# The order of the two score matmuls in a pair: turned scores first, plain scores second

## The chip, the cores and the metric

The kernel runs on one core of one Trainium2 chip. The metric is the device time of one execution in microseconds (us); the time before is the median of three runs. Five engines work in parallel and meet through semaphores: TensorE (PE in the profile; its weight loads have a row of their own, PEld), VectorE (DVE), ScalarE (ACT), GpSimd (POOL) and SyncE (SP), which here only starts DMAs.

## The reference

A transformer block on 16 sequences: an attention whose heads run along the channel axis, then a mixture of experts.

```python
# attention: x normalised over its last axis is q, ctx is k and v
qh = q.reshape(b, 8, 32, 512); kh = k.reshape(b, 8, 32, 512); vh = kh
s = SCALE * log(k_length)                      # one number per batch element
attn = softmax(s * einsum('bhdq,bhdk->bhqk', qh, kh), axis=-1)
x = x + einsum('bhqk,bhdk->bhdq', attn, vh).reshape(b, 256, 512)
# experts: normalise x, gate by softmax over 8 experts, take the top 2,
# relu(x @ w1[e]) @ w2[e] for at most C rows of each expert, weighed sum
x = x + moe(layernorm(x), Wg, w1, w2)
```

The softmax needs the maximum of each row of scores before it takes exponentials. This is why the kernel computes scores twice.

## The kernel before, in words

The attention has 32 groups (16 batch elements, two groups of 128 channels each, which are 4 heads of 32 dims). It runs in 32 steps `s`, software-pipelined over the groups:

- In step `s` the **plain** scores of group `s` are computed (queries on partitions, line 1086), 16 matmuls into a ring of three PSUM banks `ps_s`. VectorE takes the negated maximum of each (line 678), which frees the bank. The maxima are turned and sent by DMA as two extra rows into the operand `qst`.
- In the same step the **turned** scores of group `s-2` are computed (keys on partitions, line 1037), 16 matmuls into a ring of three banks `ps_t`. The extra rows subtract the maximum. ScalarE takes the exponential of each (line 460), which frees the bank.
- The exponentials are multiplied with the values (`ps_o`, line 1007, four matmuls side by side in 32-column strips) and with ones (`ps_l`, line 1013, four more) to give weighted values and sums. I call these eight the sums matmuls.

A step has four **blocks** `c` = 0 to 3 of four pairs `i` = 0 to 3. I write plain 0 to plain 3 and turned 0 to turned 3 for the matmuls of the pairs of one block. At the end of a block stand the sums matmuls for exponentials of the block before. Between pair 1 and pair 2 of a block something else may stand: in block 1 one matmul `shares` (line 1059, it takes the bank after plain 1 and waits for a small DMA `r_rows`), in block 2 the transposes of a row and of the values (lines 1044 and 1051, in the `ps_t` ring), in block 3 the gate logits (line 1109, in the `ps_s` ring) and, in odd steps from 7, the expert places (lines 1100, 1102).

The order of each engine's work is the order in which the code is written; nothing is scheduled by a planner. PE works strictly in this order. A plain matmul waits until the third-last use of the `ps_s` ring is read (`s_bank`), a turned one until the third-last use of the `ps_t` ring is read (`t_bank`). So in block 1 plain 2 waits for the maximum of plain 0, plain 3 for that of plain 1, because `shares` took a bank between them; and turned 3 waits for the exponential of turned 0. The first plain matmul of a step also waits for the DMAs that fill `qst` and `kst`, the first turned one for the DMAs with the maxima.

On ScalarE, between the exponentials of block 0 and those of block 1, stand two copies, `o_sb` from `ps_o` (line 475) and `l_sb` from `ps_l` (line 537), and then the issue of a DMA `l_wide` (line 541), which waits until `l_sb` is written. The copies wait for the sums matmuls at the end of block 0. On VectorE the maxima of a step are mixed with other short work: normalisation of a later group, the turning of the maxima, and in odd steps the choice of experts.

After step 31 a tail finishes the last two groups (turned scores only), and then the expert stage runs 16 tiles of 512 rows through `w1` and `w2`; neither has a pair that the change touches.

Of the kernel before, what the change touches and what calls it, by code (L numbers as in the profile page):

```python
# [51 lines left out]
def live(g):  # L52
    return 0 <= g < G


def pair_in(s):

    return s % 2 == 1 and 0 <= (s - 7) // 2 < B
# [45 lines left out]
def attention_and_dispatch(nc, x_rows, ctx_rows, klen, wg, out_rows, disp, totals, fill, spare,  # L104
                           w1, w2, raw, raw_ld, xin, first_ld, ident):
    s_turn, t_turn, (s_main, t_main) = bank_turns()
    with ExitStack() as stack:
# [130 lines left out]
        def turns(g, ring):  # L238

            return g // ring + 1  # L240
# [733 lines left out]
        def _(pe):  # L974
            def s_bank(k):

                if k > s_main + 2:
                    pe.wait_ge(s_free, k - 2)
                elif k > s_main:
                    pe.wait_ge(s_free, last_turn(k - s_main - 1, s_main))  # L980
                elif k > 3:
                    pe.wait_ge(s_free, k - 3)
                return s_at(k)

            def t_bank(k):

                if k > t_main + 4:
                    pe.wait_ge(t_free, k - 4)
                elif k == t_main + 4:
                    pe.wait_ge(s_free, last_turn(2, s_main))  # L990
                elif k > t_main:
                    pe.wait_ge(t_free, last_turn(k - t_main - 1, t_main))
                elif k > 3:
                    pe.wait_ge(t_free, k - 3)
                return t_at(k)

            def weighted(g, c):

                n = 4 * g + c
                pe.wait_ge(t_free, t_turn["t", g, c, HPG - 1])  # L1000
                if c == 0:
                    pe.wait_ge(t_free, t_turn["vt", g])
                    if g >= 1:
                        pe.wait_ge(o_saved, g)
                for h in range(HPG):
                    hd = slice(HD * h, HD * h + HD)
                    nc.tensor.matmul(ps_o[hd, :], vt[g % 4][:, c, hd], probs[n % 3][:, h, :],  # L1007
                                     start=(c == 0), stop=(c == NC4 - 1))
                if c == 0 and g >= 1:
                    pe.wait_ge(l_saved, g)  # L1010
                for h in range(HPG):
                    hd = slice(HD * h, HD * h + HD)
                    done = nc.tensor.matmul(ps_l[hd, :], ones[:, 0:HD], probs[n % 3][:, h, :],
                                            start=(c == 0), stop=(c == NC4 - 1))
                done.then_inc(pv_done, 1)
# [14 lines left out]
            def turned_logits(g, c, i):  # L1030
                cols = slice(P * c, P * c + P)
                if c == 0 and i == 0:
                    pe.wait_ge(mrow_ld[g % KR], (16 * 2 * NC4) * turns(g, KR))
                    if g < KR:
                        pe.wait_ge(ones_made, g + 1)
                bank = t_bank(t_turn["t", g, c, i])
                nc.tensor.matmul(bank[:], kst[g % KR][0:STACK + 2, i, cols],  # L1037
                                 qst[g % KR][0:STACK + 2, i, :], start=True, stop=True).then_inc(t_done, 1)

            def row_turned(g):  # L1040
                pe.wait_ge(x2_ready, g + 1)
                bank = t_bank(t_turn["x2t", g])
                for q in range(NC4):
                    done = nc.tensor.transpose(bank[:, P * q:P * q + P], xrow[:, g % RING, P * q:P * q + P], ident[:])
                done.then_inc(t_done, 1)

            def values(g):
                pe.wait_ge(c_ld[g % 4], 16 * turns(g, 4))
                bank = t_bank(t_turn["vt", g])
                for q in range(NC4):  # L1050
                    done = nc.tensor.transpose(bank[:, P * q:P * q + P], ct[g % 4][:, P * q:P * q + P], ident[:])
                done.then_inc(t_done, 1)

            def shares(g):
                pe.wait_ge(r_ld[g % 2], 32 * turns(g, 2))
                if g == 0:
                    pe.wait_ge(dims_st, 32)
                bank = s_bank(s_turn["r", g])
                nc.tensor.matmul(bank[:], to_dims[:], r_rows[g % 2][:], start=True, stop=True).then_inc(s_done, 1)
# [18 lines left out]
            for s in range(SLOTS):  # L1078
                for c in range(NC4):
                    for i in range(HPG):  # L1080
                        cols = slice(P * i, P * i + P)
                        if live(s):
                            if c == 0 and i == 0:
                                pe.wait_ge(stack_ld[s % KR], turns(s, KR) * (16 * COPIES))
                            bank = s_bank(s_turn["s", s, c, i])
                            nc.tensor.matmul(bank[:], qst[s % KR][0:STACK, c, cols], kst[s % KR][0:STACK, c, :],  # L1086
                                             start=True, stop=True).then_inc(s_done, 1)
                        if live(s - 2):
                            turned_logits(s - 2, c, i)
                        if i == 1 and c == 2 and live(s - 5):  # L1090
                            row_turned(s - 5)
                        if i == 1 and c == 2 and live(s - 1):
                            values(s - 1)
                        if i == 1 and c == 3 and (live(s - 5) or pair_in(s)):
                            bank = s_bank(s_turn["lp", s])
                            if pair_in(s):
                                n = (s - 7) // 2 + 1
                                pe.wait_ge(rt["before"], n)
                                pos = bank[:, 2 * E:4 * E]
                                nc.tensor.matmul(pos, earlier[:], picked[:].rearrange("p h e -> p (h e)"),  # L1100
                                                 start=True, stop=False)
                                done = nc.tensor.matmul(pos, ones[:], before[(n - 1) % 2][:].rearrange("p h e -> p (h e)"),
                                                        start=False, stop=True)
                            if live(s - 5):
                                pe.wait_ge(t_free, t_turn["x2t", s - 5])
                                if s == 5:
                                    pe.wait_ge(wg_ld, 16)
                                for q in range(NC4):
                                    done = nc.tensor.matmul(bank[:, 0:E], x2t[:, P * q:P * q + P], wg_sb[:, q, :],
                                                            start=(q == 0), stop=(q == NC4 - 1))  # L1110
                            done.then_inc(s_done, 1)
                        if i == 1 and c == 1 and live(s - 4):
                            shares(s - 4)
                    if c == 0 and live(s - 3):
                        weighted(s - 3, NC4 - 1)
                    if c > 0 and live(s - 2):
                        weighted(s - 2, c - 1)
# [742 lines left out]
```

## Time and profile before

| What | us |
|---|---|
| median of three runs | 2179.55 |
| lowest and highest run | 2177.81, 2179.68 |
| span of the profiled execution | 2177.8 |
| steady attention steps, from 80 to 605 | 525 |
| expert stage, from 681 to 2177 | 1496 |

The profile gives the span of the profiled execution, from the first to the last instruction; its own time is not listed apart from this, and the lowest run is as long as the span. Busy shares of the span: PE 97%, weight loads 70%, VectorE 46%, ScalarE 33%, GpSimd 22%. The granted TensorE clock was full (2.4 GHz) over nearly all of it.

How to read it. The start of a matmul and the time to the next start are sound; its duration is modelled and overlaps the next one, so a row of matmuls that reads 0.40 us each can follow at less than 0.25 us. A matmul needs its weight load first. When a load runs beside the matmul before, it is hidden; when it starts at the same time as its own matmul, the matmul's row is about 0.1 us longer (0.50), and that is the exposed load. The arrow names what ended an idle time.

### The profile page before, as it was taken

To read this page: it belongs to the slowest core of one execution; us is meant where nothing else is said; L and a number is where in the kernel's file an instruction comes from. 1 tells how busy PE (TensorE), PEld (TensorE's weight loads), DVE (VectorE), ACT (ScalarE), POOL (GpSimd) and SP (SyncE) were. 2 spreads that over 40 slices of the span, in tenths; PEclk is the share of its full clock that TensorE was granted. 3 is DMA by queue.
4 is the path that set the end of the run, shared out by engine and by line. 5 is a ranking of instruction groups with operands and counts; after the bars stand their busy time and mean duration, and the time that the engine had idled before them with its cause. 6 is when DMAs were issued, how large, how long until landed. Compare 5 with 4: busy or idle time off the path is not lost. (4 is left out here: it accounts for less than half of the span.)

```text
span 2177.8 us, 27085 instructions
## 1 busy us (share of the span) xinstructions
PE 2117.0 (97%) x10179; PEld 1518.8 (70%) x10179; DVE 1008.1 (46%) x1908; ACT 712.9 (33%) x1216; POOL 470.4 (22%) x593
## 2 busy tenths in 40 slices
PE   3999999999999999999999999999999999999997
PEld 1445454455547888878888887888888788888776
DVE  5677878878765434234324423423432342343211
ACT  1666666666652222113212212311311231132110
POOL 3334444343422111110301201031030102101101
PEclk9999999999999999999999999999999999999999
DMA  9876767776635435212613612422441252241101
GB/s 147 160 165 157 181 157 188 168 187 162 146 114 161 115 70 132 58 22 85 131 20 78 150 26 58 125 50 43 114 98 25 56 134 52 48 125 31 16 6 20
DMA packets 183895, 216.61 MB, mean 99 GB/s; under 512 B 39731, under 2 KB 111419, under 8 KB 183740
## 3 DMA queue, kind: packets, MB, share of 16 engines
q1 hardware_dynamic: 154128, 173.21, 34.1%
q0 software_dynamic: 22240, 37.92, 9.1%
q10 hardware_dynamic: 7372, 3.42, 0.7%
q8 instruction: 97, 1.59, 0.3%
q14 instruction: 58, 0.48, 0.1%
HBM read 113.93 MB, written 68.29 MB: 84 GB/s over the span
## 5 line engine op out<-in xcount | busy, mean ns | idle before, releaser
L1590 DVE SCALAR_TENSOR_TENSOR hlo<-ps_h,hhi 128x512 fp32r<-128x512 f32 x256 | 177.0, 692 | 928.4 <-ACT hhi L1467 928.4
L1467 ACT ACTIVATE hhi<-ps_h 128x512 fp32r<-128x512 f32 x256 | 152.9, 597 | 1123.4 <-PE ps_h L1731 1123.4
L1729 PE MATMUL ps_h<-xhi,w1hi 128*128 128x512 f32 x1024 | 404.9, 395 | 2.5 <-PEq L1316 1.3
L1748 PE MATMUL ps_y<-w2hi,hhi 128*128 128x512 f32 x1024 | 404.7, 395 | 0.7 <-DVE hlo L1590 0.7
L1749 PE MATMUL ps_y<-w2lo,hhi 128*128 128x512 f32 x1024 | 403.0, 394 | 1.0 <-issue 1.0
L1750 PE MATMUL ps_y<-w2hi,hlo 128*128 128x512 f32 x1024 | 403.7, 394 | 0.0
L1731 PE MATMUL ps_h<-xhi,w1lo 128*128 128x512 f32 x1024 | 403.6, 394 | 0.0
L1730 PE MATMUL ps_h<-xlo,w1hi 128*128 128x512 f32 x1024 | 403.0, 394 | 0.0
L678 DVE TENSOR_REDUCE nmax<-ps_s 128x1 f32<-128x512 f32 x512 | 335.7, 681 | 128.5 <-PE ps_s L1086 124.6
L460 ACT ACTIVATE probs<-ps_t 128x512 f32<-128x512 f32 x504 | 273.0, 604 | 183.1 <-PE ps_t L1037 145.8
L1729 PEld LDWEIGHTS ps_h<-xhi,w1hi 128*128 128x128 f32 x1024 | 192.3, 188 | 48.5 <-issue 3.9
L1749 PEld LDWEIGHTS ps_y<-w2lo,hhi 128*128 128x128 f32 x1024 | 193.1, 189 | 46.7 <-issue 1.5
L1730 PEld LDWEIGHTS ps_h<-xlo,w1hi 128*128 128x128 f32 x1024 | 193.0, 188 | 45.2
L1748 PEld LDWEIGHTS ps_y<-w2hi,hhi 128*128 128x128 f32 x1024 | 192.3, 188 | 46.0 <-DVE hlo L1590 1.1
L1731 PEld LDWEIGHTS ps_h<-xhi,w1lo 128*128 128x128 f32 x1024 | 192.3, 188 | 45.8
L1750 PEld LDWEIGHTS ps_y<-w2hi,hlo 128*128 128x128 f32 x1024 | 192.3, 188 | 45.8
L1086 PE MATMUL ps_s<-kst,qst 96*128 96x512 f32 x416 | 192.0, 472 | 30.5 <-DMA qst<-qlo 27.6
L1402 POOL DMA_INDIRECT out_x<-y,ids x64 | 103.3, 1614 | 453.6 <-DVE y L1632 439.0
L1086 PEld LDWEIGHTS ps_s<-kst,qst 96*128 96x128 f32 x416 | 81.7, 197 | 146.8 <-DVE nmax L678 76.7
L1037 PE MATMUL ps_t<-qst,kst 98*128 98x512 f32 x408 | 164.0, 406 | 1.9 <-DMA qst<-nturn 1.2
L1384 POOL TENSOR_TENSOR ids<-xtail,zeros 128x4 int32<-128x4 int32 x15 | 4.9, 328 | 712.8 <-DMA xtail<-dispatched 712.8
L1007 PE MATMUL ps_o<-probs,vt 128*32 128x512 f32 x1016 | 137.1, 612 | 3.3 <-ACT probs L460 3.3
(202 smaller groups left out, 2007.2 us busy)
## 6 DMA issues: line engine op xcount, KB each, us to landing
raw<-in_L_ffn_w SPq DMA_DIRECT2D x128, 512.0 KB, 4.9
qst<-qhi SPq DMA_DIRECT2D x64, 256.0 KB, 5.8
xin<-dispatched SPq DMA_DIRECT2D x60, 256.0 KB, 5.8
kst<-khi SPq DMA_DIRECT2D x52, 256.0 KB, 6.4
xt<-in_x SPq DMA_DIRECT2D x32, 256.0 KB, 3.1
ct<-in_ctx SPq DMA_DIRECT2D x32, 256.0 KB, 4.5
qst<-qlo SPq DMA_DIRECT2D x32, 256.0 KB, 6.8
xres<-in_x SPq DMA_DIRECT2D x32, 256.0 KB, 4.7
```

The lines of the kernel that those rows point to most:

```text
L460: nc.scalar.activation(probs[n % 3][:, i, :], t_at(k)[:], ACT.Exp).then_inc(t_free, 1)
L678: nc.vector.tensor_reduce(nmax[s % 2][:, i, c:c + 1], s_at(k)[:], AX, ALU.max, negate=True).then_inc(s_free, 1)
L1037: nc.tensor.matmul(bank[:], kst[g % KR][0:STACK + 2, i, cols], qst[g % KR][0:STACK + 2, i, :], start=True, stop=True).then_inc(t_done, 1)
L1086: nc.tensor.matmul(bank[:], qst[s % KR][0:STACK, c, cols], kst[s % KR][0:STACK, c, :], start=True, stop=True).then_inc(s_done, 1)
L1467: nc.scalar.activation(hhi[k % 2][:], ps_h[k % 3][:], ACT.Relu).then_inc(hhi_ready, 1)
L1590: nc.vector.scalar_tensor_tensor(hlo[k % 2][:], ps_h[k % 3][:], 0.0, hhi[k % 2][:].bitcast(F32), ALU.max, ALU.subtract).then_inc(h_ready, 1)
L1729: nc.tensor.matmul(to, w1hi[:, c, fs], xhi[n % 2][:, c, :], start=(c == 0), stop=False)
L1730: nc.tensor.matmul(to, w1hi[:, c, fs], xlo[n % 2][:, c, :], start=False, stop=False)
L1731: done = nc.tensor.matmul(to, w1lo[:, c, fs], xhi[n % 2][:, c, :], start=False, stop=(c == NC4 - 1))
L1748: nc.tensor.matmul(ps_y[b][:], hhi[k % 2][:, bs], w2hi[:, f, :], start=(f == 0), stop=False)
L1749: nc.tensor.matmul(ps_y[b][:], hhi[k % 2][:, bs], w2lo[:, f, :], start=False, stop=False)
L1750: done = nc.tensor.matmul(ps_y[b][:], hlo[k % 2][:, bs], w2hi[:, f, :], start=False, stop=(f == NF - 1))
```

## The change

In each pair of the step loop, the turned matmul now stands ahead of the plain one. The wait for `stack_ld` moves with the plain matmul. Nothing else is moved: the matmuls and transposes between pairs 1 and 2, and the sums matmuls at a block's end, stand where they stood; the rings' numbering is as before, since the two rings are counted apart. The other engines' programs are the same.

```diff
                         cols = slice(P * i, P * i + P)
+                        if live(s - 2):
+                            turned_logits(s - 2, c, i)
                         if live(s):
                             if c == 0 and i == 0:
                                 pe.wait_ge(stack_ld[s % KR], turns(s, KR) * (16 * COPIES))
                             bank = s_bank(s_turn["s", s, c, i])
                             nc.tensor.matmul(bank[:], qst[s % KR][0:STACK, c, cols], kst[s % KR][0:STACK, c, :],
                                              start=True, stop=True).then_inc(s_done, 1)
-                        if live(s - 2):
-                            turned_logits(s - 2, c, i)
```

PE in step 8, block 1, before. The numbers are buffer numbers: `ps_s1` is the second bank of the plain ring, `ps_t2` the third of the turned ring, `qst3` the operand of group 8, `qst1` that of group 6.

```order
L1013 MATMUL ps_l<-probs2,ones 32x512 x4
L1086 MATMUL ps_s1<-kst3,qst3 128x512
L1037 MATMUL ps_t2<-qst1,kst1 128x512
L1086 MATMUL ps_s2<-kst3,qst3 128x512
L1037 MATMUL ps_t0<-qst1,kst1 128x512
L1059 MATMUL ps_s0<-r_rows0,to_dims 128x512
L1086 MATMUL ps_s1<-kst3,qst3 128x512
L1037 MATMUL ps_t1<-qst1,kst1 128x512
L1086 MATMUL ps_s2<-kst3,qst3 128x512
L1037 MATMUL ps_t2<-qst1,kst1 128x512
L1007 MATMUL ps_o<-probs0,vt2 32x512 x4
```

The same place in the changed kernel:

```order
L1013 MATMUL ps_l<-probs2,ones 32x512 x4
L1037 MATMUL ps_t2<-qst1,kst1 128x512
L1088 MATMUL ps_s1<-kst3,qst3 128x512
L1037 MATMUL ps_t0<-qst1,kst1 128x512
L1088 MATMUL ps_s2<-kst3,qst3 128x512
L1059 MATMUL ps_s0<-r_rows0,to_dims 128x512
L1037 MATMUL ps_t1<-qst1,kst1 128x512
L1088 MATMUL ps_s1<-kst3,qst3 128x512
L1037 MATMUL ps_t2<-qst1,kst1 128x512
L1088 MATMUL ps_s2<-kst3,qst3 128x512
L1007 MATMUL ps_o<-probs0,vt2 32x512 x4
```

Each turned matmul moved one place up and each plain one down, within its pair. The block now begins with a turned matmul and has plain 3 between turned 3 and the sums matmuls. (Line 1086 of before is line 1088 after.)

PE in step 8, block 3, before:

```order
L1086 MATMUL ps_s1<-kst3,qst3 128x512
L1037 MATMUL ps_t0<-qst1,kst1 128x512
L1086 MATMUL ps_s2<-kst3,qst3 128x512
L1037 MATMUL ps_t1<-qst1,kst1 128x512
L1109 MATMUL ps_s0<-wg_sb,x2t 128x8 x4
L1086 MATMUL ps_s1<-kst3,qst3 128x512
L1037 MATMUL ps_t2<-qst1,kst1 128x512
L1086 MATMUL ps_s2<-kst3,qst3 128x512
L1037 MATMUL ps_t0<-qst1,kst1 128x512
L1007 MATMUL ps_o<-probs2,vt2 32x512 x4
```

And in the changed kernel:

```order
L1037 MATMUL ps_t0<-qst1,kst1 128x512
L1088 MATMUL ps_s1<-kst3,qst3 128x512
L1037 MATMUL ps_t1<-qst1,kst1 128x512
L1088 MATMUL ps_s2<-kst3,qst3 128x512
L1109 MATMUL ps_s0<-wg_sb,x2t 128x8 x4
L1037 MATMUL ps_t2<-qst1,kst1 128x512
L1088 MATMUL ps_s1<-kst3,qst3 128x512
L1037 MATMUL ps_t0<-qst1,kst1 128x512
L1088 MATMUL ps_s2<-kst3,qst3 128x512
L1007 MATMUL ps_o<-probs2,vt2 32x512 x4
```

The logits keep their place; again turned 3 (bank `ps_t0`) now stands ahead of plain 3 (bank `ps_s2`).

## Rows read from the trace of the kernel before

**Rows 1.** Windows: steady attention steps, and the expert stage; columns stand first

```profile
core 0: us, PE busy (x) PEld busy (x) DVE busy (x) ACT busy (x) POOL busy (x), PEclk, DMA share, GB/s
80.00:605.00 525.00, 521.68 (x3200) 259.88 (x3192) 417.10 (x1037) 337.23 (x639) 215.04 (x332) 1.00 0.71 165
681.00:2177.00 1496.00, 1480.48 (x6384) 1193.87 (x6384) 500.20 (x643) 318.84 (x478) 205.32 (x173) 1.00 0.33 72
```

**Rows 2.** Waits of weight loads, 80 to 615 us: total, times, longest

```profile
PEld ps_s L1086 <- DVE nmax L678: 79.3, 124, 0.8
PEld ps_t L1037 <- ACT probs L460: 2.7, 12, 0.3
```

**Rows 3.** Timeline, PE, step 22: start, us, engine, line, operation, shape, count

```profile
429.90 1.04 PE L1013 MATMUL ps_l<-probs,ones 128*32 128x512 f32 x8
...
430.87 0.50 PE L1086 MATMUL ps_s<-xin,qst 96*128 96x512 f32 x1
431.21 0.40 PE L1037 MATMUL ps_t<-qst,kst 98*128 98x512 f32 x1
431.44 0.39 PE L1086 MATMUL ps_s<-xin,qst 96*128 96x512 f32 x1
...
432.41 0.50 PE L1086 MATMUL ps_s<-xin,qst 96*128 96x512 f32 x1
...
433.44 0.50 PE L1037 MATMUL ps_t<-qst,kst 98*128 98x512 f32 x1
433.87 1.06 PE L1007 MATMUL ps_o<-probs,vt 128*32 128x512 f32 x8
```

**Rows 4.** Timeline, weight loads, step 22, block 1: plain 3 and turned 3

```profile
433.05 0.19 PEld L1086 LDWEIGHTS ps_s<-xin,qst 96*128 96x128 f32 x1 [0.34 <-DVE nmax L678]
433.44 0.19 PEld L1037 LDWEIGHTS ps_t<-qst,kst 98*128 98x128 f32 x1 [0.20 <-ACT probs L460]
```

**Rows 5.** Timeline, ScalarE and its DMA issue, step 22, block 1

```profile
431.01 0.60 ACT L475 ACTIVATE o_sb<-ps_o 128x512 f32<-128x512 f32 x1 [1.22 <-PE ps_l L1013]
...
432.12 0.57 ACTq L541 DMA_DIRECT2D l_wide<-l_sb  x1
432.79 2.07 ACT L460 ACTIVATE probs<-ps_t 128x512 f32<-128x512 f32 x4 [0.70 <-ACT l_sb L537]
```

**Rows 6.** Timeline, VectorE, step 22, block 1: the first two maxima

```profile
431.46 0.68 DVE L678 TENSOR_REDUCE nmax<-ps_s 128x1 f32<-128x512 f32 x1
...
432.34 0.65 DVE L678 TENSOR_REDUCE nmax<-ps_s 128x1 f32<-128x512 f32 x1
```

**Rows 7.** Timeline, several engines, step 21, block 1

```profile
410.93 1.04 PE L1013 MATMUL ps_l<-probs,ones 128*32 128x512 f32 x8
...
413.59 0.66 DVE L678 TENSOR_REDUCE nmax<-ps_s 128x1 f32<-128x512 f32 x1
413.83 2.07 ACT L460 ACTIVATE probs<-ps_t 128x512 f32<-128x512 f32 x4 [0.71 <-ACT l_sb L537]
...
414.30 0.19 PEld L1086 LDWEIGHTS ps_s<-kst,qst 96*128 96x128 f32 x1 [0.54 <-DVE nmax L678]
...
414.48 0.19 PEld L1037 LDWEIGHTS ps_t<-qst,kst 98*128 98x128 f32 x1
...
414.96 1.07 PE L1007 MATMUL ps_o<-probs,vt 128*32 128x512 f32 x8
```

**Rows 8.** Timeline, several engines, step 22, block 3

```profile
441.12 0.69 DVE L678 TENSOR_REDUCE nmax<-ps_s 128x1 f32<-128x512 f32 x1 [0.57 <-PE ps_s L1086]
...
443.06 0.19 PEld L1086 LDWEIGHTS ps_s<-xin,qst 96*128 96x128 f32 x1 [0.35 <-DVE nmax L678]
...
443.71 1.07 PE L1007 MATMUL ps_o<-probs,vt 128*32 128x512 f32 x8
```

**Rows 9.** Timeline, weight load, step 5, block 1: last plain

```profile
113.60 0.19 PEld L1086 LDWEIGHTS ps_s<-kst,qst 96*128 96x128 f32 x1 [0.56 <-DVE nmax L678]
```

**Rows 10.** Timeline, PE, step 2: first turned matmul

```profile
54.22 0.80 PE L1037 MATMUL ps_t<-qst,kst 98*128 98x512 f32 x1 [1.24 <-DMA qst<-nturn]
```

## The prediction, made before the changed kernel ran

> **What bounds the kernel now.** I read the windows first, to see which stage can move at all. The expert stage lasts 1496 us and holds no pair [rows 1]; it keeps its time. The pairs stand in the attention. From 80 to 605 us PE is busy for 521.68 of 525 us, VectorE for 417 and ScalarE for 337 [rows 1]. So PE sets the pace there, and a step (18.8 us) is the sum of PE's start-to-start distances. The change adds no work; it can only move places where PE waits.
>
> Next the waits of the weight loads. Plain loads waited for VectorE's maxima 124 times, 79.3 us together; turned loads for ScalarE's exponentials 12 times, 2.7 us [rows 2]. The first number looks like a reward for sending a turned matmul ahead. It isn't one: a load that waits while the matmul before it runs costs nothing, and the loads at the head of a block wait behind the sums matmuls anyway. I therefore read the timeline of PE, block by block, for distances above the usual. Usual are 0.34 for a matmul with an exposed load (430.87 to 431.21), 0.23 for one with a hidden load (431.21 to 431.44) [rows 3], so an exposed load costs 0.11; and 0.43 from an exposed matmul to the sums matmuls (433.44 to 433.87) [rows 3], which is 0.32 from a hidden one.
>
> Blocks 0 and 2 run at these distances. Block 1 doesn't. In step 22, from the second half of block 0's sums matmuls (429.90) to block 1's sums matmuls (433.87) pass 3.97 us [rows 3]; in step 21 the same stretch is 410.93 to 414.96, 4.03 us [rows 7]. Without waits it would be 0.97 to the first matmul, 1.54 to plain 2 [rows 3], then 0.34 + 0.23 + 0.23 + 0.32, so 3.63. Two things hold it. Plain 3's load starts at 433.05 when plain 1's maximum is read (432.34 + 0.65) [rows 4, 6]. Turned 3's load starts at 433.44, released by ScalarE [rows 4]: turned 0's exponential started at 432.79 [rows 5], and 0.65 later its bank is free. In step 21 it is the same 0.65, from 413.83 to 414.48 [rows 7].
>
> What sets that exponential decides everything. It started late not because its scores were late (turned 0 started at 431.21 [rows 3]) but because ScalarE stood behind `o_sb`, `l_sb` and the issue of `l_wide`: 431.01, 432.12 to 432.69, then 432.79, with the idle time before put down to `l_sb` [rows 5]. That chain starts from the sums matmuls of block 0, ahead of all pairs of block 1. From 429.90 to 432.79 are 2.89 us; from 410.93 to 413.83 are 2.90 [rows 3, 5, 7]. It is a fixed anchor: sending turned 0 earlier doesn't move it.
>
> **The change part by part, block 1, even steps.** Turned 2 takes plain 2's place at 432.41 [rows 3], plain 2 follows at 432.75, and turned 3 could go at 432.98. But its bank is free only at 433.44, as before. PE waits there, and now plain 3 is queued behind it, where before plain 3 went ahead and filled part of the wait. After: turned 3's load 433.44, plain 3 at + 0.34, sums matmuls at + 0.32, so 434.10 against 433.87: 0.23 lost. Is plain 3 itself ready at 433.78? Plain 0 and 1 come 0.23 later, so the maxima too: plain 1's is read at about 433.23 [rows 6], in time. There are 12 such steps (6 to 30 without 24; the 12 waits of rows 2 are nearly these): 2.8 us.
>
> **Block 1, odd steps.** Before, plain 3's load started at 414.30 (VectorE), turned 3's at 414.48 in its shadow [rows 7]. After: 414.48 + 0.34 + 0.32 = 415.14 against 414.96: 0.18 lost. Plain 1's maximum, 413.59 + 0.66 + 0.23 = 414.48 [rows 7], is in time. 12 steps (7 to 29): 2.1 us. Steps 3 and 31 behave like even ones in my reading: 0.5 us.
>
> **Exceptions.** In step 5 VectorE was late for another reason, plain 3's load came at 113.60 [rows 9]. There the last load then stands at 113.60 + 0.43 to the sums, against 113.60 + 0.34 + 0.32: 0.23 gained. Steps 4 and 24 had late inputs too and come out at 0. Block 1 together: 2.8 + 2.1 + 0.5 - 0.2 = 5.2 us.
>
> **Block 3, even steps.** Plain 3 waits for plain 1's maximum (load at 443.06), and sums matmuls start at 443.71 [rows 8]. VectorE sat idle for plain 0 there (0.57 [rows 8]), so all its work shifts by 0.23 with the arrival: plain 3's load at 443.29, sums at + 0.43 = 443.72. That is 0.01 or 0.02 in 13 steps, 0.2 us. If VectorE had slack the same place would gain up to 0.22 (down to 443.50).
>
> **Step starts.** In step 2 the first turned matmul waited until 54.22 for the maxima's DMA [rows 10], and the plain one had gone ahead of it; now it queues behind. At most one matmul at that low speed (0.80 by its row), at least nothing, since ScalarE and VectorE waited for PE soon after; I take 0.2 us. From step 3 on both inputs are there long before.
>
> **What goes for nothing.** The stall of `shares` on its DMA lies ahead of the ScalarE anchor and stays hidden. The tail sees plain 3 of step 31 come 0.23 us later on VectorE, where it waits for PE afterwards: nothing.
>
> **Sum.** 5.2 + 0.2 + 0.2 = 5.6 us on the span of 2177.8, which is as long as the lowest run; the median is 1.8 above. On the median: 2185.1 us.
>
> **A rule against the size.** The row: in step 22 turned 3's load did not start before its wait was over, and it was exposed [rows 4]. The Trainium skill, "TensorE: Matmul & The Clock Gate", step-by-step part, says that PE pulls weight loads ahead of matmuls in flight, matmuls keeping their order. Were the load of a waiting matmul pulled ahead, the 0.11 would vanish from the changed block, and by the rule the sum would be about 3 us. This trace disagrees for a load whose bank isn't free: the wait holds the load too.
>
> **Rivals.**
> - Half the price. If the load of the waiting turned 3 were done ahead, 24 blocks lose 0.11 less: 5.6 - 2.6 = 3.0 us, 2182.6. Near it lies the case in which only VectorE counts: even blocks would then go 433.05 + 0.23 + 0.43 = 433.71, 0.16 gained, odd ones nothing: -2 us, 2177.6. Against both: the releaser ACT in rows 2 and 4. Together 0.20.
> - Faster. The wait of plain 3 is covered by turned 3, and no bank of the turned ring is late: 3.63 instead of 3.97 or 4.03 in 28 steps, 10.4 us, 2169.2. For it: 124 waits for VectorE against 12 for ScalarE. It decides from the point where turned 0's exponential is done by 432.98, 0.46 sooner than it is. Nothing in the change moves the chain before it. 0.09.
> - Slower than I say. Every plain matmul reaches VectorE 0.23 later, and a block without interludes has no slack: plain 0 to the slot of plain 3's load is five distances of 0.23, 1.17; its own 0.40, the maximum 0.68 [rows 3, 6] and two handovers of 0.05 (432.99 to 433.05 is one [rows 4, 6]) are 1.18. If block 0 slips by 0.1 in 29 steps, that is 2.9 us more, 2188.0. For it: nothing to spare. Against: before, both ends stood at the same distance. 0.15.
> - My forecast, 0.56, of its own range 2183 to 2187.
>
> **Range and chances.** No change is what this kernel's measurement can't tell from it, 0.2% or 4.4 us: 2175.2 to 2183.9. Faster 0.10 (the faster rival and a little). Same 0.22 (the half price and a low end of mine). Slower 0.68. The range reaches from 2179 to 2189, which leaves out the faster rival and extremes.
>
> **What would show it.** In the changed profile the stretch between the sums matmuls in block 1 should be 4.2 us in even and odd steps alike; turned 3's load in block 1 released by ACT in nearly every step from 6 on; waits of turned loads for ACT at some 25, and more than 2.7 us; blocks 0 and 2 as long as before. If that stretch is 3.7, ScalarE wasn't the anchor and I am wrong in sign. If it is 4.1, the load was hidden. If block 0 grew, the last rival is at work.

## The result and the profile after

| | median, us | runs | ratio to before [95%] |
|---|---|---|---|
| before | 2179.55 | 5 (2177.8 to 2182.7) | 1 |
| after | 2190.76 | 5 (2182.4 to 2194.7) | 1.0041 [1.0023, 1.0060] |

The change makes the kernel slower: by the ratio 0.41% or 8.9 us (2179.55 x 0.0041), by its interval 5.0 to 13.1 us. The forecast was 5.6 us. One execution of the study, of t_first_l_sb_later, ran at a granted clock of 0.66 and took 2981.31 us; it counts in the median given there, not in the ratio. A run's time is 1.7 to 1.8 us above the span of the same execution (after: 2182.37 and 2180.6), so before's profile, with a span of 2177.8, is of an execution at its median, not of its lowest run. The profiled execution of after was the shortest of its five runs, with a span only 2.8 us longer than before's. So the profile can't be read by its span alone; I cut both spans at the same four instructions:

| Stretch, us | before | after | difference |
|---|---|---|---|
| start to the first matmul of step 3 | 72.34 | 71.11 | -1.2 |
| from there to the last sums matmuls of step 31 | 542.00 | 546.66 | +4.7 |
| from there to the first expert matmul (tail) | 67.53 | 64.41 | -3.1 |
| expert stage | 1495.9 | 1498.4 | +2.5 |

The second line is the one that holds the changed pairs in their steady form. The windows show PE waiting more in it. The view is the windows of after, in the columns of [rows 1]; the middle window is part of the tail.

```profile
core 0: us, PE busy (x) PEld busy (x) DVE busy (x) ACT busy (x) POOL busy (x), PEclk, DMA share, GB/s
80.00:605.00 525.00, 516.96 (x3172) 256.20 (x3168) 407.33 (x1023) 337.34 (x633) 212.83 (x331) 1.00 0.70 165
616.00:681.00 65.00, 55.28 (x391) 33.01 (x390) 38.72 (x125) 26.02 (x51) 23.31 (x36) 0.98 0.41 142
681.00:2177.00 1496.00, 1483.22 (x6386) 1192.43 (x6384) 500.03 (x643) 319.75 (x478) 207.95 (x173) 1.00 0.33 72
```

In the steady steps PE is busy for 516.96 us where it was for 521.68 in the same 525 us [rows 1], so 4.7 us more are waiting. Where, the waits of after's weight loads and turned matmuls tell (80 to 615 us; total, times, longest):

```profile
PEld ps_t L1037 <- issue: 78.0, 113, 0.8
PEld ps_t L1037 <- ACT probs L460: 43.0, 56, 0.8
...
PE ps_t L1037 <- ACT probs L460: 7.0, 25, 0.3
...
PEld ps_s L1088 <- DVE nmax L678: 4.5, 13, 0.3
```

Against [rows 2], the plain loads' 124 waits for VectorE shrank to 13, as the order suggests, and the turned loads' waits for ScalarE grew from 12 to 56. By their places in the timeline, 27 of the 56 are turned 3's in block 1; the other 29 are turned 0's in block 3, hidden behind the sums matmuls (block 3 is no longer than before). The matmuls themselves waited for ScalarE 25 times, 7.0 us, all of them turned 3 in block 1, and never in before. The 79.3 us of the plain loads are not gained: the load at the head of a block still waits behind the sums matmuls, it is only a turned one now (78.0 us, put down to issue). PE in step 22, block 1, of after, in the columns of [rows 3]:

```profile
431.70 1.04 PE L1013 MATMUL ps_l<-probs,ones 128*32 128x512 f32 x8
...
432.68 0.50 PE L1037 MATMUL ps_t<-qst,kst 98*128 98x512 f32 x1
433.02 0.40 PE L1088 MATMUL ps_s<-xin,qst 96*128 96x512 f32 x1
...
434.23 0.50 PE L1037 MATMUL ps_t<-qst,kst 98*128 98x512 f32 x1
434.57 0.40 PE L1088 MATMUL ps_s<-xin,qst 96*128 96x512 f32 x1
435.24 0.50 PE L1037 MATMUL ps_t<-qst,kst 98*128 98x512 f32 x1 [0.28 <-ACT probs L460]
435.58 0.40 PE L1088 MATMUL ps_s<-xin,qst 96*128 96x512 f32 x1
435.91 1.06 PE L1007 MATMUL ps_o<-probs,vt 128*32 128x512 f32 x8
```

From the sums matmuls of block 0 (431.70) to those of block 1 (435.91) are 4.21 us, 3.97 before [rows 3]. Turned 3 has idle time ahead of it that ScalarE ended, its row is 0.50 (the load lies open), and plain 3 follows 0.34 later. The loads in the same place, to be laid beside [rows 4]:

```profile
435.24 0.19 PEld L1037 LDWEIGHTS ps_t<-qst,kst 98*128 98x128 f32 x1 [0.72 <-ACT probs L460]
435.35 0.19 PEld L1088 LDWEIGHTS ps_s<-xin,qst 96*128 96x128 f32 x1
```

Before, plain 3's load came first, at its own release by VectorE, and 0.39 later turned 3's. Now turned 3's load waits 0.72 and plain 3's comes right behind it. ScalarE in the same block, beside [rows 5]:

```profile
432.81 0.60 ACT L475 ACTIVATE o_sb<-ps_o 128x512 f32<-128x512 f32 x1 [1.46 <-PE ps_l L1013]
433.31 0.59 ACT L537 ACTIVATE l_sb<-ps_l 128x512 f32<-128x512 f32 x1
433.93 0.56 ACTq L541 DMA_DIRECT2D l_wide<-l_sb  x1
434.59 1.57 ACT L460 ACTIVATE probs<-ps_t 128x512 f32<-128x512 f32 x3 [0.70 <-ACT l_sb L537]
```

The first exponential starts at 434.59, which is 2.89 us after the sums matmuls (431.70), as before, although its scores were started 0.98 after them (432.68) instead of 1.31. VectorE was not what was waited for (plain 1's maximum ends at 434.38 + 0.65 = 435.03, before turned 3's release):

```profile
434.38 0.65 DVE L678 TENSOR_REDUCE nmax<-ps_s 128x1 f32<-128x512 f32 x1
...
435.56 1.27 DVE L678 TENSOR_REDUCE nmax<-ps_s 128x1 f32<-128x512 f32 x2
```

By block, the stretch from sums matmuls to sums matmuls, medians over steps 6 to 31, us:

| | block 0 | block 1 even | block 1 odd | block 2 | block 3 even | block 3 odd |
|---|---|---|---|---|---|---|
| before | 3.05 | 3.98 | 4.04 | 3.99 | 4.11 | 4.38 |
| after | 3.05 | 4.21 | 4.22 | 3.97 | 4.11 | 4.38 |

Only block 1 is longer. Twelve even steps by 0.23, twelve odd ones by 0.18, and step 24 (+0.04) and 31 (+0.23) are 5.2; steps 3 to 5 together are 0; block 2 gives back 0.02 in 26 steps, 0.5. The sum is the +4.7 of the table. What differs at the ends of the span does not follow the order: in the fourteen traces of this study the tail took 64.2 to 67.5 us and the expert stage 1495.9 to 1500.3, and before's own values are the longest tail and the shortest expert stage of all.

### The profile page after: what moved, and what is told of

Its sections match the earlier page's. It is cut to its first block and busy times, and to the rows that moved or that the text cites. A ratio compares the mean times of both kernels' runs of the same rounds, so it can differ in the third digit from the quotient of the medians.

```text
span 2180.6 us, 27085 instructions
## 1 busy us (share of the span) xinstructions
PE 2111.4 (97%) x10179; PEld 1510.5 (69%) x10179; DVE 1001.5 (46%) x1908; ACT 716.6 (33%) x1216; POOL 472.6 (22%) x593
## 5 line engine op out<-in xcount | busy, mean ns | idle before, releaser
L1088 PE MATMUL ps_s<-kst,qst 96*128 96x512 f32 x416 | 173.6, 428 | 29.2 <-DMA qst<-qlo 27.8
L1037 PE MATMUL ps_t<-qst,kst 98*128 98x512 f32 x408 | 181.9, 450 | 11.2 <-ACT probs L460 6.5
L1037 PEld LDWEIGHTS ps_t<-qst,kst 98*128 98x128 f32 x408 | 77.6, 191 | 121.0 <-issue 64.0
```

## The experiments

Theory A is the forecast's: ScalarE's two copies and its DMA issue hold turned 3 of block 1, and plain 3 queues behind it. Rival B: the loss lies outside block 1, in other blocks, at the step starts, in the tail or the experts. Rival C: what costs is that VectorE gets its plain scores 0.23 us later. Rival D, for the last pair of edits: block 1 has a floor above the sum of its distances. Beside them stands a doubt, that part of the time is the measurement's. Three groups ran, each on a chip of its own and each beside more runs of before (medians 2183.59, 2181.97 and 2183.99 us).

### First group: the changed kernel again, and its parts

**t_first_again**: the changed kernel, unedited.

> The changed kernel once more, beside before. Theory A (only block 1 got longer, by 5.2 us in all; the rest of the measured 9 us is chance in the clock's level and in the pace of the expert stage): block 1 is 4.21 us from sums matmuls to sums matmuls in every step from 6 on, the start of step 31's first matmul lies 3 to 6 us behind that of before (596.4), and the median is 4 to 12 us above before with a wider spread than before. Rival B (something outside block 1 grew for good, in the tail or the expert stage): the same matmul distance of 0.233 us in the expert stage shows again from the first tiles on, and the stretch from step 31 to the first expert matmul is longer than before's.

Measured: 2190.66 us, ratio 1.0038 [1.0022, 1.0055]. The result repeats. Block 1 is 4.22 in even and odd steps. One expectation missed: the first matmul of step 31 stood at 609.6, 13.2 us behind that of before (596.4) where 3 to 6 were expected, so in this execution block 1 is less than half of the delay. Rival B's signs in the tail and the experts did not come: the tail was shorter than before's (65.1 against 67.5) and the expert pace changed between its two values. Something else showed: step 3's first turned matmul waited for the DMA of the maxima (start, us, engine, line, operation, shape, idle before):

```profile
69.28 1.04 PE L1013 MATMUL ps_l<-probs,ones 128*32 128x512 f32 x8
72.37 0.50 PE L1037 MATMUL ps_t<-qst,kst 98*128 98x512 f32 x1 [2.05 <-DMA qst<-nturn]
```

**plain_first_in_block1**: the new order everywhere but in block 1 (the edit is against the changed kernel).

```diff
-                        if live(s - 2):
+                        if live(s - 2) and (c != 1):
                             turned_logits(s - 2, c, i)
                         if live(s):
 ...
+                        if live(s - 2) and not (c != 1):
+                            turned_logits(s - 2, c, i)
```

> Turned first in blocks 0, 2 and 3, plain first in block 1. Theory A: block 1 goes back to 3.97 us in even and 4.03 in odd steps, the other blocks stay, so the attention is as long as before within 1 us and the time is that of before within 0.1%. Rival B (the new order costs in each block or at each step start): most of the loss stays, 5 us or more above before.

Measured: 2189.45, ratio 1.0029 [1.0015, 1.0042]. Block 1 is back at 4.05 and 4.04. The time is not back: the median is 5.9 us over before's, where theory A has at most 0.1% and rival B 5 us or more. Two things are in the trace. Block 3 of even steps took 4.41 instead of 4.11, and step 3 went as follows:

```profile
72.50 0.67 PE L1037 MATMUL ps_t<-qst,kst 98*128 98x512 f32 x1 [1.90 <-DMA qst<-nturn]
72.97 0.63 PE L1088 MATMUL ps_s<-kst,qst 96*128 96x512 f32 x1
73.39 0.63 PE L1037 MATMUL ps_t<-qst,kst 98*128 98x512 f32 x1
```

The wait again, and then rows of 0.63 at distances of 0.43 until 75.5. The granted clock of this stretch and of the same one in the run before it:

```profile
72.00:76.00 4.00, 3.50 (x8) 2.38 (x8) 2.20 (x4) 2.02 (x4) 1.40 (x1) 0.58 1.05 264
```

```profile
72.00:76.00 4.00, 3.63 (x24) 1.86 (x24) 2.86 (x5) 2.06 (x4) 1.09 (x1) 1.00 1.04 256
```

0.58 against 1.00: one block ran near the lower level (1.2 GHz) after PE had waited for 1.90 us, and the other, after 2.05 us of wait, at the upper. Block 0 of step 3 took 6.53 us here, 5.16 in t_first_again, 3.05 in steady steps.

**turned_first_only_pair3_block1**: before's order, with turned first in one pair of sixteen, pair 3 of block 1 (again against the changed kernel).

```diff
-                        if live(s - 2):
+                        if live(s - 2) and (c == 1 and i == 3):
                             turned_logits(s - 2, c, i)
 ...
+                        if live(s - 2) and not (c == 1 and i == 3):
+                            turned_logits(s - 2, c, i)
```

> Plain first everywhere except in the last pair of block 1. Theory A (turned 3 waits for ScalarE, plain 3 is queued behind it): block 1 is 4.21 us, as in the changed kernel, in even and odd steps; the attention loses the whole 5 us with 1 pair in 16 turned round. Rival C (the loss is the shift of VectorE's work by 0.23 us, which needs plain 0 and 1 late): VectorE isn't late here, so block 1 stays below 4.10.

Measured: 2190.07, ratio 1.0030 [1.0018, 1.0042]. PE in step 8, block 1:

```profile
166.99 1.04 PE L1013 MATMUL ps_l<-probs,ones 128*32 128x512 f32 x8
...
169.51 0.50 PE L1088 MATMUL ps_s<-kst,qst 96*128 96x512 f32 x1
169.85 0.39 PE L1037 MATMUL ps_t<-qst,kst 98*128 98x512 f32 x1
170.54 0.50 PE L1037 MATMUL ps_t<-qst,kst 98*128 98x512 f32 x1 [0.30 <-ACT probs L460]
170.88 0.40 PE L1088 MATMUL ps_s<-kst,qst 96*128 96x512 f32 x1
171.21 1.06 PE L1007 MATMUL ps_o<-probs,vt 128*32 128x512 f32 x8
```

4.22 us from 166.99 to 171.21: this one pair carries the whole lengthening of block 1, since turned 3 waits for ScalarE and plain 3 for turned 3. That refutes rival C, which had it below 4.10. Nothing waits at step 3 (block 0 takes 3.05).

**t_first_l_sb_later**: the changed kernel, and ScalarE's `l_sb` copy with its `l_wide` issue moved behind the first exponential of block 1.

```diff
 (scalar engine, in the pair loop, ahead of the second exponential of block 1)
+                        if (c, i) == (1, 0) and live(s - 3):
+                            g = s - 3
+                            ...
+                            nc.scalar.activation(l_sb[g % 2][:], ps_l[:], ACT.Copy).then_inc(l_saved, 1)
+                            act.wait_ge(l_saved, g + 1)
+                            ...
+                            act.dma_start(l_wide[g % 2][:], ...).then_inc(l_ld[g % 2], 16)
 (the same lines removed behind o_sb)
```

> The changed kernel, and on ScalarE the copy l_sb and the issue of l_wide stand behind the first exponential of block 1 instead of ahead of it. Theory A: ScalarE no longer holds turned 3; VectorE's maximum of plain 1 holds plain 3 instead: block 1 about 3.8 us in even steps and 4.04 in odd ones instead of 4.21, so 8 us less than the changed kernel and 1 to 3 us less than before. Rival C (VectorE's shift is what costs): block 1 stays at 4.2 and the time is that of the changed kernel.

Measured: 2185.86, ratio 1.0010 [1.0000, 1.0021]; block 1 is 3.81 in even and 4.04 in odd steps. ScalarE, then PE's loads, step 22:

```profile
437.49 0.60 ACT L475 ACTIVATE o_sb<-ps_o 128x512 f32<-128x512 f32 x1 [1.46 <-PE ps_l L1015]
437.98 0.59 ACT L460 ACTIVATE probs<-ps_t 128x512 f32<-128x512 f32 x1
438.46 0.60 ACT L510 ACTIVATE l_sb<-ps_l 128x512 f32<-128x512 f32 x1
```

```profile
439.25 0.19 PEld L1039 LDWEIGHTS ps_t<-qst,kst 98*128 98x128 f32 x1
439.76 0.19 PEld L1090 LDWEIGHTS ps_s<-xin,qst 96*128 96x128 f32 x1 [0.33 <-DVE nmax L680]
```

The exponential now starts at 437.98, 1.60 after the sums matmuls (436.38) instead of 2.89; turned 3's load no longer waits, and plain 3's is now the late one, for VectorE. Theory A's anchor is the copy `l_sb` and the issue of `l_wide`; no run takes one of the two away alone. The time missed its expectation: 1 to 3 us below before were expected, it came out 2.3 above (median against median). Block 1 is together shorter than in before's trace, but block 0 of odd steps is together about 4 us longer and block 3 of even steps about 3; the third group comes back to these.

### Second group: a copy of before, and the second hold

**plain_first_unchanged**: the kernel before, unedited, timed like the others.

> The kernel before as a control, since the kernels of the last group showed waits in block 3 of even steps (4.1 to 4.8 us) and block 0 of odd steps (3.0 to 3.9) that the two first traces don't have. If they belong to the chip or the moment (what I expect), they are here too, and the ratio to before is 1.000 within 0.15%. If they belong to an order with turned matmuls first, block 3 is 4.1 us here and block 0 is 3.05.

Measured: 2186.57, ratio 1.0017 [1.0005, 1.0030]. A copy of the kernel before came out 0.17%, 3.7 us, above the kernel before, and its interval does not reach 1. So a single ratio here can be off by about that much, and the expectation (within 0.15%) just missed. Block 3 of even steps is 4.11 and block 0 is 3.05 here. By the words of the expectation that speaks for the order as the cause of the longer ones; but t_first_both_later, below, has turned first in every pair and, on this same chip, 4.11 and 3.05 too.

**plain_first_l_sb_later**: the kernel before with the ScalarE move alone.

> Plain first in every pair, and ScalarE's l_sb copy and l_wide issue behind the first exponential of block 1. Theory A: turned 3's load is hidden behind plain 3 and starts with it; VectorE holds plain 3 as in the kernel before. Block 1: 433.05 + 0.34 + 0.32 - 429.90 = 3.81 in even, 4.03 in odd steps, the same as turned first with the same edit (3.81 and 4.04). So with ScalarE's hold gone the order of a pair is worth 0, and 2 us less than before. Rival C (turned first costs by VectorE's shift): this one is 0.2 us a block faster than its twin with turned first.

Measured: 2178.80, ratio 0.9985 [0.9973, 0.9997]; block 1 is 3.82 and 4.05, as with turned first. With ScalarE out of the way both orders give the same block 1, and VectorE sets it. That answers rival C once more. The times of the two (2185.86 on the first chip, 2178.80 here) differ by more than the order explains: the pairs' stretch, cut as in the first table, took 550.97 us there and 538.90 here, with block 1 alike.

**t_first_both_later**: t_first_l_sb_later, and on VectorE three short pieces (the turning of the maxima, the sums of the gates, the variance of a later group) moved behind the second maximum of block 1.

```diff
-                        if (c, i) == (1, 0) and live(s - 1):
+                        if (c, i) == (1, 1) and live(s - 1):
 ...
-                        if (c, i) == (1, 0) and pair_in(s):
+                        if (c, i) == (1, 1) and pair_in(s):
 ...
-                        if (c, i) == (1, 0) and live(s + 2):
+                        if (c, i) == (1, 1) and live(s + 2):
```

> Turned first, ScalarE as in the run with l_sb later, and on VectorE the turning of the maxima, the variance and the sums of the gates behind the maximum of plain 1 in block 1, not ahead of it. Theory A: both holds are gone, block 1 falls to the 3.63 us that its matmuls need, 0.35 to 0.4 less than before in each of 29 steps: 10 us less than before. Rival D (block 1 has a floor that the sum of distances does not see): it stays at 3.8 or above.

Measured: 2168.43, ratio 0.9943 [0.9927, 0.9959], 12.4 us faster than before. Block 1 is 3.67 in both kinds of steps. PE in step 22:

```profile
420.14 1.04 PE L1015 MATMUL ps_l<-probs,ones 128*32 128x512 f32 x8
...
422.68 0.50 PE L1039 MATMUL ps_t<-qst,kst 98*128 98x512 f32 x1
423.02 0.39 PE L1090 MATMUL ps_s<-xin,qst 96*128 96x512 f32 x1
423.25 0.39 PE L1039 MATMUL ps_t<-qst,kst 98*128 98x512 f32 x1
423.48 0.39 PE L1090 MATMUL ps_s<-xin,qst 96*128 96x512 f32 x1
423.80 1.07 PE L1009 MATMUL ps_o<-probs,vt 128*32 128x512 f32 x8
```

From 420.14 to 423.80, 3.66 us: 0.34, 0.23, 0.23 and 0.32 at the end, the block without waits that the prediction worked out as 3.63. Rival D's floor is not there.

**plain_first_both_later**: the ScalarE move and the VectorE move in before's order.

> Plain first, with both edits. Theory A: block 1 at 3.63 as with turned first, within 0.05; total within 1 us of its twin and some 10 us less than before. If the turned-first twin is faster by 2 us or more, the order has a worth of its own once ScalarE doesn't hold it.

Measured: 2170.42, ratio 0.9944 [0.9927, 0.9961], block 1 3.66 and 3.66. The ratios are the same; the medians, of six and five runs, lie 2.0 us apart, where 1 was expected. Between the two traces the pairs' stretch differs by 4.4 us (530.90 with turned first, 535.33 here), and that is one place: in step 25 the small DMA `r_rows` came late, PE waited 1.38 us, the granted clock from 480 to 488 us was 0.57, and blocks 1 and 2 took 6.04 and 5.34. Without the two holds the order in the pair is worth nothing that can be measured. These two are the fastest kernels of the study.

### Third group: repeats on a third chip

> The kernel before as a control beside the next three on one chip. Ratio to before 1.000, within 0.2% by chance alone (the first control gave 1.0017). Whether block 3 of even steps is 4.1 us or more here decides whose the waits of the first group were: 4.1 on every kernel of this group, or longer on every one, and they are the chip's.

> The changed kernel: block 1 at 4.21 us; 5 us over the control, give or take 2.

> Turned first outside block 1. Theory A: as the control within 0.15%, block 1 back at 4.0. Rival B (turned first has a price outside block 1, as the first run of this kernel, 0.3% over before, would have it): again 0.25% or more over the control, with a block other than 1 longer than in the control.

> Turned first in the last pair of block 1 alone. Theory A: block 1 at 4.21, all of the changed kernel's loss, 5 us over the control and as far over the kernel with plain first in block 1.

| kernel (edit as above) | median, us | ratio to before [95%] | block 1 even, odd | block 3 even | step 3, block 0 |
|---|---|---|---|---|---|
| plain_first_control_2 | 2187.30 | 1.0012 [0.9997, 1.0028] | 3.98, 4.04 | 4.11 | 3.05 |
| t_first_third | 2195.48 | 1.0047 [1.0030, 1.0063] | 4.21, 4.22 | 4.47 | 4.72 |
| plain_first_in_block1_2 | 2188.36 | 1.0025 [1.0013, 1.0037] | 4.05, 4.05 | 4.46 | 6.50 |
| turned_first_only_pair3_block1_2 | 2192.00 | 1.0033 [1.0020, 1.0046] | 4.22, 4.22 | 4.11 | 3.05 |

The pattern repeats. Taking the two copies of before as zero (mean 1.0015), the changed kernel's three ratios (mean 1.0042) leave 0.27% or 6.0 us, the one pair's two (mean 1.0032) 3.7 us, and the order outside block 1 (mean 1.0027) 2.7 us. Each ratio has a half-interval of 0.12 to 0.19%, 3 to 4 us, so these three are rough. Against the copy of before on the same chip alone, the medians are 8.2 us more for the changed kernel (5, give or take 2, expected), 4.7 for the one pair (5 expected) and 1.1 for the order outside block 1 (theory A, within 0.15%, holds by the time; rival B's 0.25% did not come). The one pair is 3.6 us over the kernel with plain first in block 1. The traces fix block 1's 5.2 us far better than the times do.

**The wait at step 3.** It stands in 5 of 7 traces with turned first at step 3, 1.0 to 2.05 us long, and in none of 7 with plain first. But turned-first kernels also come to step 3 sooner: in t_first_again the sums matmuls before it stand at 69.28, in before at 71.37. The first matmul of step 3 stood at 70.8 to 73.0 in the seven turned-first traces (mean 71.9), and at 70.2 to 72.3 in the seven others (mean 71.8). What is gained up to the DMA is lost at it. A net cost is seen only where PE then ran slowly, in the two plain_first_in_block1 traces (6.53 and 6.50 against 5.16, 1.4 us).

**What moves a copy of the same kernel.** The stretch from step 3 to the end of step 31 took 542.00 us in before's profile, 547.81 in plain_first_unchanged and 555.68 in plain_first_control_2, all the same program. In the last, PE stood once for 5 us:

```profile
191.59 0.79 PE L1059 MATMUL ps_s<-r_rows,to_dims 8*128 8x512 f32 x1 [5.04 <-DMA r_rows<-r_hl]
```

The small DMA for `shares` came late. The longer even block 3 has another look. In t_first_third, step 22, VectorE first, then ScalarE and its DMA queue:

```profile
449.94 0.69 DVE L678 TENSOR_REDUCE nmax<-ps_s 128x1 f32<-128x512 f32 x1 [1.16 <-issue]
```

```profile
449.91 0.60 ACT L460 ACTIVATE probs<-ps_t 128x512 f32<-128x512 f32 x1 [1.97 <-PE ps_t L1037]
449.97 1.98 ACTq L521 DMA_DIRECT2D r_rows<-r_hl  x2
```

VectorE starts this maximum after 1.16 us of idle time for which the view names no releaser, and 0.03 us before it ScalarE starts the first exponential of the block, also late: 1.28 us after the start of its matmul (448.63), where both before and after have 0.43 to 0.54 in all such blocks. So in this block both engines start on the first scores late, at the same moment, and plain 3 and the sums matmuls are late with them. A long issue of the DMAs alone doesn't make it: in before the same two took 2.02 us in step 26 (516.89), and block 3 was 4.10.

The table's medians hide how often this happens. Block 3 of even steps (there are fourteen, 4 to 30) is above 4.2 us in 7 to 12 steps in the five kernels of the first and third chip with turned first in block 3, in 8 steps in turned_first_only_pair3_block1, and in 4 steps each in its repeat and in plain_first_control_2 (5.48 in step 30), which is before itself. Block 0 of odd steps from 5 on is above 3.15 us in these same eight traces, too, in 1 to 9 steps. In before, in after and in all four kernels of the second chip neither happens once, and one of these, t_first_both_later, has turned first everywhere. So the order alone doesn't make these delays. They came more often with it on the third chip (7 and 10 steps against 4 and 4), and whether it adds to them is not settled: each trace is one execution.

## Why the prediction was right in sign and short in size

- **What bounds the kernel; the anchor.** Right. The exponential starts 2.89 us after the sums matmuls in after as in before [rows 3, 5], and with turned first moving `l_sb` and `l_wide` moved it to 1.60. Block 1 fell with it in both orders (3.81 and 3.82 in even steps), so the hold is shown by taking it away.
- **Block 1, even and odd, + 0.23 and + 0.18.** Right: 3.98 to 4.21 and 4.04 to 4.22, turned 3 released by ScalarE in after's block 1 in 27 loads and 25 matmuls ("some 25"); the 56 of the view count block 3 as well.
- **Exceptions.** Right in kind: step 3 4.01 to 4.25, step 5 4.47 to 4.23, step 31 3.98 to 4.21; steps 4 and 24 within 0.05. Block 1 together is 5.2 us as forecast.
- **Block 2** was taken as unchanged. It gave back 0.02 a step, 0.5 us, which the forecast did not have.
- **Block 3, even.** In before and after 4.11 both: 0.0 where 0.2 was forecast. It was longer in other executions, see above.
- **Step starts.** At step 2 the forecast held: the second plain matmul stood at 54.82 before, and the first at 55.02 now, 0.20 later. "From step 3 on both inputs are there long before" was false. The maxima's DMA is the last input at step 3; in before, turned 0 came at 72.69 and so didn't meet it. Net, this moved the start of step 3 by nothing that I can show. PE in after at step 2, beside [rows 10]:

```profile
54.43 0.80 PE L1037 MATMUL ps_t<-qst,kst 98*128 98x512 f32 x1 [4.68 <-DMA qst<-nturn]
55.02 0.63 PE L1088 MATMUL ps_s<-xin,qst 96*128 96x512 f32 x1
```

- **The rule against the size.** The row first: turned 3's load in after starts at 435.24, with its matmul and after its wait, and the next matmul stands 0.34 on. The Trainium skill, "TensorE: Matmul & The Clock Gate", step-by-step part, has PE pull loads ahead of matmuls in flight. For a load whose wait isn't over the trace disagrees, as in before: block 1 would else be 4.10, and it is 4.21.
- **Rivals.** Half the price, VectorE only, and faster all fell with block 1 at 4.21; the faster one became true only when both holds were taken away (3.67). Block 0 stayed at 3.05 in before and after, so it did not slip, and the 1.17 against 1.18 held.
- **Sum and range: held, by a narrow margin.** The sum of 5.6 us is inside the interval of the measured change (5.0 to 13.1), and the pairs' stretch grew by 4.7. By the ratio the changed kernel is at 2188.5 us (2179.55 + 8.9), 0.5 below the top of the range; the plain median of its five runs, 2190.76, is 1.8 above it. Both lie outside the 2183 to 2187 of the forecast itself, and 2188.5 is close to the 2188.0 of the rival "Slower than I say", whose mechanism (block 0 slips) was absent. That the range held owes something to chance. Its bounds allowed for terms of the kernel and little for how well three runs place a median. The same kernel's medians later were 2182.0 to 2184.0 and, as a copy, 2186.6 and 2187.3; its pairs' stretch alone varied by 13.7 us between executions. The 3.3 us between 5.6 and 8.9 are of the size by which the two copies of before missed it with no change at all (3.7 and 2.6 us). Both copies came out above it: if that is an offset that every kernel here carries, the change is 6.0 us, close to the sum. Whether the order outside block 1 adds some of the 3.3, through the DMAs at step 3 and the delays of blocks 3 and 0, stays open.
- **The span.** The sum starts from "the span of 2177.8, which is as long as the lowest run". That reading was wrong: the profiled execution was one at the median, and its span is 1.7 to 1.8 us below its time, as in every run here. The 1.8 that were added make up for it, so the 2185.1 is right for another reason than the one given.

## What to carry to other kernels

Before two queued instructions change places, find for each the wait that ends last and what that wait hangs on: if it hangs on something that the order can't move (here ScalarE's copies and DMA issue), the one with the fixed wait belongs last, so that the other fills the gap. Don't count waits: of before's 124 waits for VectorE most lengthened no block, and the 12 for ScalarE were just the even steps in which it set block 1; the distances between PE's starts tell which. And taking away the holds was worth more than their order: moving ScalarE's copy and DMA issue gave 3.3 us by the ratio, with VectorE's three pieces moved too it was 12 us in either order, and then the order no longer mattered.

## What the runs showed of the hardware

- Expert matmuls follow at one of two paces, 0.2319 or 0.2331 us each, all at a granted clock of 1.00, and the pace changes a few times in an execution. In before it was the faster one until about 1690 us, in after the slower one from about 970 to 1700 and again from about 1890 on. Over 6144 matmuls the full difference is 7.4 us. What picks the pace is not known.
- In step 2 matmuls follow at 0.43 us with rows of 0.63 while the granted-clock column says 1.00; the change to 0.23 came at 59.7 to 60.1 us in after and at 61 to 63 in before. The count of matmuls from 60 to 62 us shows it, 8 rows in before and 16 in after:

```profile
60.00:62.00 2.00, 2.00 (x8) 0.69 (x10) 1.60 (x3) 1.49 (x4) 0.94 (x3) 1.00 1.06 150
```

```profile
60.00:62.00 2.00, 2.00 (x16) 0.86 (x19) 1.88 (x5) 1.73 (x4) 0.98 (x3) 1.00 1.05 147
```

- In the tail the granted clock differed between executions: 0.91, 0.70 and 0.79 in before over 640 to 660, 660 to 670 and 670 to 680 us, 1.00, 1.00 and 0.90 in after. I put most of the 3.1 us of the tail down to it: of the fourteen traces the three with a tail above 66 us (66.9 to 67.5) have a mean granted clock of 0.90 to 0.92 in it, and ten of the eleven others 0.95 to 0.98. No run isolates it.
- Issuing a DMA from ScalarE's queue took 0.56 us for `l_wide`, and for the two of `r_rows` 1.98 us in t_first_third (step 22) but 1.14 in plain_first_control_2 (step 30); in before alone it varied from 1.11 to 2.02 us, in steps whose block 3 was equally long.
- The small DMA of `r_rows` can land 5 us late in a kernel that meets it without a wait in most steps; over 80 to 615 us `shares` waited for it 1.6 us in before and 6.7 in plain_first_control_2, the same program.
